# Layer 1's table products in a two-layer cross-attention kernel: two 64-row tiles of the array in place of a block-diagonal operand

## The reference, cut to what matters

```
a = layer_norm(ctx)                      # 64 keys per batch
K = a @ Wk.T ; V = a @ Wv.T              # 16 heads of 64
scores = (x @ Wq.T) K^T / 8              # per head
out = softmax(scores) V @ Wo.T
return x + tanh(gate) * out
```

## Time and profile before

| | us |
|---|---|
| median of 3 runs | 1936.01 (1934.52 to 1938.28) |
| the profiled execution, device time | 1932.28 |
| its span | 1930.5 |
| PE busy in the span | 1826.7 (95%) |
| DVE, ACT, POOL busy | 1082.6, 585.9, 1032.3 |

### The profile page before, as it was taken

How to read it: one execution, slowest core, us unless ns; L and a number is a source line. 1 busy time by engine, 2 the same in 40 slices (tenths; PEclk the granted TensorE clock), 3 DMA queues, 4 the chain that set the end, 5 groups by cost and what they waited for, 6 DMA issues and landing times.

```text
span 1930.5 us, 22356 instructions
## 1 busy us (share of the span) xinstructions
PE 1826.7 (95%) x8640; PEld 1509.4 (78%) x8640; DVE 1082.6 (56%) x1086; ACT 585.9 (30%) x680; POOL 1032.3 (53%) x580
## 2 busy tenths in 40 slices
PE   5999999999988899999999977999999999999998
PEld 5788888888876777888778856887788778877887
DVE  6888888888867444444344456335633563356342
ACT  3444444444434332233332323112211221122111
POOL 2677777777758755465544656225522552255221
PEclk9999999999999999999999989999999999999999
DMA  8423333233163475655756554422342234132110
GB/s 204 108 76 82 83 79 78 74 81 85 45 191 111 131 235 201 198 180 175 242 188 211 189 189 153 152 77 83 136 153 66 100 118 153 66 118 101 66 55 33
DMA packets 249961, 244.43 MB, mean 127 GB/s; under 512 B 61440, under 2 KB 204928, under 8 KB 249856
## 3 DMA queue, kind: packets, MB, share of 16 engines
q1 hardware_dynamic: 248704, 241.97, 39.9%
q10 hardware_dynamic: 1152, 1.05, 0.2%
HBM read 157.99 MB, written 84.93 MB: 126 GB/s over the span
## 4 chain that ended last, share of the span: by engine, by line
PE 56%; DVE 19%; issue 9%; ACT 6%; POOL 4%; DMA 3%; SPq 2%; ACTq 0%; DVEq 0%; POOLq 0%
PE ps L53 18%; PE ps L55 18%; PE ps L54 18%; DVE small L972 4%; DVE pr L995 3%; ACT pr L741 3%; DVE pT1r L1006 2%; DVE pT0r L1006 2%; PE ps L648 2%; ACT ot L735 2%; DVE xT0r L902 1%; DVE xT1r L902 1%; POOL prob L1280 1%; DVE x2r L1075 1%; DMA xb<-in_x_dram 1%
## 5 line engine op out<-in xcount | busy, mean ns | idle before, releaser
L1275 POOL TENSOR_TENSOR prob<-prob,small 128x1024 f32<-128x1024 f32 x32 | 61.0, 1908 | 397.0 <-DVE small L1086 397.0
L1206 POOL TENSOR_TENSOR pr<-pr,small 128x1024 f32<-128x1024 f32 x64 | 122.0, 1906 | 100.0 <-DVE small L1001 100.0
L1082 DVE SCALAR_TENSOR_TENSOR prob<-ps,bias 128x1024 f32<-128x1024 f32 x32 | 39.1, 1222 | 227.6 <-PE ps L55 227.6
L840 ACT CAST x2Th<-x2r 128x1024 fp32r<-128x1024 f32 x32 | 33.6, 1050 | 424.6 <-DVE x2r L1075 424.6
L1227 POOL TENSOR_TENSOR xb<-xb,bo 128x1024 f32<-128x1024 f32 x32 | 79.9, 2497 | 141.0 <-DMA xb<-in_x_dram 141.0
L1201 POOL TENSOR_TENSOR pr<-pr,small 128x1024 f32<-128x1024 f32 x64 | 124.0, 1938 | 34.8 <-DVE small L976 34.6
L1050 DVE TENSOR_TENSOR y<-ps,xb 128x512 f32<-128x512 f32 x64 | 44.0, 687 | 159.3 <-PE ps L55 156.4
L972 DVE TENSOR_REDUCE small<-pr 128x16 f32<-128x1024 f32 x64 | 78.1, 1220 | 91.0 <-ACT pr L741 91.0
L53 PE MATMUL ps<-wo0h,oc0l 128*128 128x512 f32 x256 | 101.6, 397 | 0.0
L53 PE MATMUL ps<-wo0h,oc1l 128*128 128x512 f32 x256 | 101.0, 395 | 0.0
L53 PE MATMUL ps<-xT0h,wq0l 128*128 128x512 f32 x256 | 100.7, 393 | 0.0
(11 more groups left out here) (320 smaller groups left out, 5583.1 us busy)
## 6 DMA issues: line engine op xcount, KB each, us to landing
o_scratch<-ot SPq DMA_DIRECT2D x256, 64.0 KB, 1.8
ocr<-o_scratch SPq DMA_DIRECT2D x16, 1024.0 KB, 6.2
xb<-in_x_dram SPq DMA_DIRECT2D x32, 512.0 KB, 6.0
x_scratch<-y SPq DMA_DIRECT2D x32, 512.0 KB, 3.5
a_scratch<-ost SPq DMA_DIRECT2D x64, 256.0 KB, 3.0
b_scratch<-ost SPq DMA_DIRECT2D x64, 256.0 KB, 2.5
xd<-x_scratch SPq DMA_DIRECT2D x128, 128.0 KB, 2.8
raw<-b_scratch SPq DMA_DIRECT2D x32, 512.0 KB, 8.0
```

The lines of the kernel that those rows point to most:

```text
L1206: nc.gpsimd.tensor_tensor(heads(v), heads(v), mx.unsqueeze(2).to_broadcast([P, TPB * GRP, KEYS]), ALU.subtract)\
L1275: nc.gpsimd.tensor_tensor(prob[:], prob[:], mx1.unsqueeze(2).to_broadcast([P, H1, KEYS]), ALU.subtract)\
```

## The change

The two heads of a pair are no longer put in one product with zeros. `bd` holds only the blocks, [128, BATCH, KEYS]: partitions 0 to 63 are head 0, 64 to 127 head 1. Each product is issued as two matmuls over 64 partitions each, one per head, alternating, into separate banks. The 16 products of a pair f become 8 rounds r: r < 4 makes two column tiles e of table A (per e: 3 terms x 2 heads, 256 columns each), r >= 4 makes two batches and half of Wo's columns of table B (3 terms x 2 heads, 512 columns each). A round has two banks, and the rounds alternate between V and TT, so four banks are used; before writing, a round waits for the evictions of the round before the last. ACT evicts head 0's bank and DVE head 1's, for r < 4 with a strided write that puts the heads side by side. The transposes into TT and the first scores wait for the evictions, and round 1 for Wo's turned rows. `diagonal` is one instruction instead of two; POOL's zeroing and its wait go. The stores keep their number and size.

```diff
-        bd = [[at(f"bd{i}{x}", 180 + 4 * i + 2 * j, [P, BATCH, 2, KEYS], F32R) for j, x in enumerate("hl")]
+        bd = [[at(f"bd{i}{x}", 180 + 4 * i + 2 * j, [P, BATCH, KEYS], F32R) for j, x in enumerate("hl")]
-        ost = [at(f"ost{i}", 188 + 2 * i, [P, HALF]) for i in range(4)]
+        ost = [at(f"ost{i}", 188 + 4 * i, [P, 2, HALF]) for i in range(2)]
-        X = V
+        X = [V, [TT[:, HALF * i:HALF * (i + 1)] for i in range(2)]]
...
@@ store_outer
-                sp.wait_ge(evac_d if o % 2 else evac_a, 8 * f + o // 2 + 1)
+                tile = ost[o // 2 % 2][:, o % 2]
+                if i == 0 or o % 2 == 0:
+                    sp.wait_ge(evac_a, 8 * f + o // 2 + 1)
+                if i == 0 or o % 2 == 1:
+                    sp.wait_ge(evac_d, 8 * f + o // 2 + 1)
...
@@ table_part, s == 0
-                        after(pe, wo1_lo, f)
+                        after(pe, evac_a, 8 * f)
+                        after(pe, evac_d, 8 * f)
@@ table_part, s >= 3
-                    for o in range(4 * (s - 3), 4 * (s - 2)):
...
+                    for r in range(2 * (s - 3), 2 * (s - 2)):
+                        if r == 0:
                             pe.wait_ge(o_ev, UNITS)
                             pe.wait_ge(bd_lo, 2 * f + 1)
                             pe.wait_ge(w1_lo, f + 1)
+                        if r in (1, 4):
                             pe.wait_ge(bd_lo, 2 * f + 2)
                             pe.wait_ge(wo1_lo, f + 1)
-                        after(pe, evac_d if o % 2 else evac_a, 8 * f + o // 2)
-                        if i == 0:
-                            a_ = [wqs[x][:, e] for x in (0, 1)]
-                            b_ = [bd[0][x][:].rearrange("p b h s -> p (b h s)") for x in (0, 1)]
-                        else:
-                            a_ = [bd[1][x][:, e // 2].rearrange("p h s -> p (h s)") for x in (0, 1)]
-                            b_ = [woT[x][:, HALF * (e % 2):HALF * (e % 2 + 1)] for x in (0, 1)]
-                        three(nc, X[o % 2], a_, b_, True, True).then_inc(outer, 1)
+                        after(pe, evac_a, 8 * f + r - 1)
+                        after(pe, evac_d, 8 * f + r - 1)
+                        head = [slice(HD1 * h, HD1 * (h + 1)) for h in range(2)]
+                        terms = ((1, 0), (0, 1), (0, 0))
+                        for e in range(2 * r, 2 * r + 2) if r < 4 else ():
+                            for j, (x, y_) in enumerate(terms):
+                                for h in range(2):
+                                    last = nc.tensor.matmul(X[r % 2][h][:, CTX * (e % 2):][:, :CTX], wqs[x][head[h], e],
+                                                            bd[0][y_][head[h]].rearrange("p b s -> p (b s)"),
+                                                            start=j == 0, stop=j == 2)
+                                    if e % 2 == 1 and j == 2:
+                                        last.then_inc(outer, 1)
+                        for j, (x, y_) in enumerate(terms) if r >= 4 else ():
+                            q, n = divmod(r - 4, 2)
+                            for h in range(2):
+                                last = nc.tensor.matmul(X[r % 2][h], bd[1][x][head[h], 2 * q:2 * q + 2].rearrange("p b s -> p (b s)"),
+                                                        woT[y_][head[h], HALF * n:HALF * (n + 1)], start=j == 0, stop=j == 2)
+                                if j == 2:
+                                    last.then_inc(outer, 1)
...
@@ ACT out_slot
-                    for o in range(4 * (s - 3), 4 * (s - 2), 2):
-                        act.wait_ge(outer, 16 * f + o + 1)
-                        after(act, ost_st[o % 4], 16 * (4 * f + o // 4))
-                        nc.scalar.copy(ost[o % 4][:], X[0]).then_inc(evac_a, 1)
+                    for r in range(2 * (s - 3), 2 * (s - 2)):
+                        act.wait_ge(outer, 16 * f + 2 * r + 1)
+                        for i in range(2 if r < 4 else 1):
+                            after(act, ost_st[2 * (r % 2) + i], 16 * (4 * f + r // 2))
+                        if r < 4:
+                            nc.scalar.copy(ost[r % 2][:].rearrange("p e (b h s) -> p e b h s", b=BATCH, h=2)[:, :, :, 0],
+                                           X[r % 2][0].rearrange("p (e b s) -> p e b s", e=2, b=BATCH)).then_inc(evac_a, 1)
+                        else:
+                            nc.scalar.copy(ost[r % 2][:, 0], X[r % 2][0]).then_inc(evac_a, 1)
...
@@ POOL slot
-                if u == UNITS + 3:
-                    pool.wait_ge(pv, UNITS)
-                    for i in range(2):
-                        for x in range(2):
-                            nc.gpsimd.memset(f32(bd[i][x][:]), 0.0).then_inc(bd_zero, 1)
```

More of the change, by code:

```diff
@@ L182, in program @@
         (wo_hi, wo_lo, c_ld, oc_hi, oc_lo, o_done, xbo, y_done, st_done, aggr, coef, applied, scaled, normed,
-         bd_zero, wt_turned, wT_hi, wT_lo, w1_hi, w1_lo, wo1_turned, wo1_hi, wo1_lo, proj, bd_hi, bd_lo, outer, evac_a,
+         wt_turned, wT_hi, wT_lo, w1_hi, w1_lo, wo1_turned, wo1_hi, wo1_lo, proj, bd_hi, bd_lo, outer, evac_a,
          evac_d) = (sem(n) for n in (
-             "wo_hi wo_lo c_ld oc_hi oc_lo o_done xbo y_done st_done aggr coef applied scaled normed bd_zero "
+             "wo_hi wo_lo c_ld oc_hi oc_lo o_done xbo y_done st_done aggr coef applied scaled normed "
              "wt_turned wT_hi wT_lo w1_hi w1_lo wo1_turned wo1_hi wo1_lo proj bd_hi bd_lo outer evac_a evac_d").split())
@@ L308, in store_outer @@
                 i, e = divmod(o, 8)
-                sp.wait_ge(evac_d if o % 2 else evac_a, 8 * f + o // 2 + 1)
+                tile = ost[o // 2 % 2][:, o % 2]
[3 more added lines that the diff above has]
+                    sp.wait_ge(evac_d, 8 * f + o // 2 + 1)
                 if i == 0:
                     sp.dma_start(d["a"][:, P * e:P * (e + 1), P * f:P * (f + 1)].rearrange("b p c -> p b c"),
-                                 ost[o % 4][:].rearrange("p (b c) -> p b c", b=BATCH)).then_inc(ost_st[o % 4], 16)
+                                 tile.rearrange("p (b c) -> p b c", b=BATCH)).then_inc(ost_st[o % 4], 16)
                 else:
-                    b, n = divmod(e, 2)
-                    sp.dma_start(d["b"][b, P * f:P * (f + 1), HALF * n:HALF * (n + 1)], ost[o % 4][:])\
+                    q, n = divmod(e // 2, 2)
+                    rows = P * f + HD1 * (o % 2)
+                    sp.dma_start(d["b"][2 * q:2 * q + 2, rows:rows + HD1, HALF * n:HALF * (n + 1)], tile)\
                         .then_inc(ost_st[o % 4], 16)
@@ L587, in table_part @@
                 else:
-                    for o in range(4 * (s - 3), 4 * (s - 2)):
-                        i, e = divmod(o, 8)
-                        if o == 0:
+                    for r in range(2 * (s - 3), 2 * (s - 2)):
+                        if r == 0:
                             pe.wait_ge(o_ev, UNITS)
@@ L593, in table_part @@
                             pe.wait_ge(w1_lo, f + 1)
-                        if o == 8:
+                        if r in (1, 4):
                             pe.wait_ge(bd_lo, 2 * f + 2)
                             pe.wait_ge(wo1_lo, f + 1)
-                        after(pe, evac_d if o % 2 else evac_a, 8 * f + o // 2)
-                        if i == 0:
-                            a_ = [wqs[x][:, e] for x in (0, 1)]
-                            b_ = [bd[0][x][:].rearrange("p b h s -> p (b h s)") for x in (0, 1)]
-                        else:
-                            a_ = [bd[1][x][:, e // 2].rearrange("p h s -> p (h s)") for x in (0, 1)]
-                            b_ = [woT[x][:, HALF * (e % 2):HALF * (e % 2 + 1)] for x in (0, 1)]
-                        three(nc, X[o % 2], a_, b_, True, True).then_inc(outer, 1)
+                        after(pe, evac_a, 8 * f + r - 1)
[17 more added lines that the diff above has]
+                                    last.then_inc(outer, 1)
             def logits(u):
@@ L608, in logits @@
                 if u == 0:
-                    pe.wait_ge(wo1_lo, KT)
+                    pe.wait_ge(evac_a, 8 * KT)
+                    pe.wait_ge(evac_d, 8 * KT)
                 if u == 1:
@@ L778, in diagonal @@
                 after(act, outer, 16 * (f - 1) + 8 * (i + 1))
[L779 to L782, removed]
+                nc.scalar.copy(bd[i][0][:].rearrange("p b (r i) -> p b r i", r=2),
+                               PJ[i].rearrange("p (r b i) -> p b r i", r=2, b=BATCH)).then_inc(bd_hi, 1)
             def out_slot(h):
@@ L787, in out_slot @@
                     act.wait_ge(pv, UNITS)
-                    act.wait_ge(bd_zero, 4)
                 f, s = table(h - 1)
@@ L1020, in diagonal @@
                 dve.wait_ge(bd_hi, 2 * f + i + 1)
[L1021 to L1025, removed]
+                nc.vector.tensor_tensor(bd[i][1][:].rearrange("p b (r i) -> p b r i", r=2),
```

(11 more changed lines are left out.)

## The result

The changed kernel takes 2126.44 us (median of 4 runs, 2123.12 to 2128.39), the kernel before 1935.59: a ratio of 1.099, 95% interval 1.0974 to 1.1006. The forecast was 1914.8, in a range of 1888 to 1934.

The account below looks back on a forecast made before the run. PE was taken to bound the table stage, busy 474.8 of 477 us. Outer parts falling from 104.4 to 82.9 us gave 21.5, less 0.3 waited away at the stage's end: 1936.0 - 21.2 = 1914.8 us, range 1888 to 1934.

Parts of the forecast that it names:

- Stores keep their bytes.: Clause on the table stores, listed among the edits that cost nothing: 0 us.
- D: Rival: the tiles' matmuls run one after the other, plus mode changes; 3 us more, 1939; chance 0.12.
- E: Rival: each alternation between tiles empties the array like a mode change; 67 us more, 2003; chance 0.04.
- The stalls: In each outer part, PE's eviction waits of 0.55 us (table A) and 0.38 (table B) go with four banks.
- Columns: Outer-part matmul time: from no overlap, 2.88 (table A) and 2.73 us (B), to full overlap, 1.44 and 1.36.
- Weight loads: In outer parts, the tiles' loads pass one after the other: table A 2.72 us a part, table B 1.36.
- rival B: The tiles also load beside each other, table A parts at 1.44 us; 42 us less, 1894.3; chance 0.26.
- Rival C: A load waits until its own tile's matmul is over, table B parts 2.0 us; 11 less, 1925; chance 0.12.
- The changes of mode: Switching between whole array and tiles, twice a part, 64 times: 0.275 us each, 0.55 a part, 17.6 in all.
- The sum on PE: All 32 outer parts on PE: 82.9 us against 104.4, 21.5 less.
- None is near: In the table stage no other engine is close to having no slack; POOL, the busiest other, has 45% idle.
- A: The forecast itself: tiles multiply side by side, loads pass one after the other; 1914.8 us, chance 0.40.

Follow-up runs that it names:

- f2: Changed kernel with the values' columns in the order key, batch, so a table B store has 64 keys outermost and 2 batches inside: 1909.57 us.
- f3: Kernel before, each table B product stored to 64 rows of two batches instead of 128 rows of one: 2155.57 us.
- f6: Kernel before, each table B product stored to 32 rows of all four batches, outermost dimension 4: 2004.15 us.
- g1: f2 with POOL computing the layer norm's coefficients before the low part of the next chunk instead of after: 1888.72 us.
- f4: Kernel before, still block-diagonal operands and whole-array matmuls, but products go round four banks (V and TT) instead of two: 1918.15 us.
- f5: f2 with the three products of one head issued before the three of the other instead of alternating, both tables: 1910.71 us.
- f7: g1 with the six matmuls of one head of a table A round issued before the six of the other: 1894.42 us.

## Why the prediction was wrong

*The step that failed* is one clause among the edits costed at nothing: "Stores keep their bytes." They do, and their shape changed. From the diff, one line of `store_outer`, it could have been asked what the row of a store's dimensions says: 128 rows, against 2 x 64. The price is shown from three sides: the changed kernel without the slow shape is 217 us faster (f2), the old kernel with it is 221 us slower (f3), and with half as slow a shape 70 us slower (f6). The Trainium skill has the rule (DMA: Bandwidth & Descriptors, Why a DMA increments its semaphore by 16 and not by 1): a DMA is spread over the largest number of engines up to 16 that divides the size of the slowest dimension (of those larger than 1) on both of its sides; the shares of 0.13 and 0.26 of 16 engines agree. The prediction weighed pages on TensorE alone.

*Where the time went.* From 645 us to the first scores, the changed kernel takes 687.8 us (to 1332.75) and g1, which has the same matmuls, 454.6 (to 1099.62). Of these 233 us, 163 are PE's idle time in the stage, 33 the longer wait before the first scores (46.8 against 13.9), and 37 are the same matmuls at a lower clock (478.0 us busy against 440.7).

My slower rivals, D and E, put the loss on PE. Of the sentence on what would prove me wrong, "if PE waited for another engine in the stage", the wait came, but by the transposes more than by round 1: PE waited 15.3 us for `bd1l` before round 1, three times, and 100.1 for `ost`. "The transposes at s = 0 wait for round 7's evictions, which have a half tile too" was the sentence that failed with the stores.

*The stalls*: right. f4 alone gave 16.7 us against 17. But the list of DVE's work beside them (residual, statistics and two copies, under 3 us) leaves out the multiplication by gamma, which waits for ACT.

*Columns*: the halving is shown in both tables. The upper bound, no overlap, is out.

*Weight loads*: wrong by 20.5 us, on the good side. I let the tiles' loads pass one after the other, 2.72 us for a part of A; it took 1.62 with its way out. In the timeline with PE's loads (PEld), the two tiles' loads are one row, and the next pair of loads comes 0.11 later:

```profile
680.69 0.19 PEld L609 LDWEIGHTS ps<-bd0h,wqsl 64*128 64x128 f32 x2 [0.35 <-issue]
680.80 0.19 PEld L609 LDWEIGHTS ps<-bd0l,wqsh 64*128 64x128 f32 x2
```

That is rival B's mechanism, which I gave 0.26. The 0.11 us of the earlier trace rows was the time of a load on one tile, and I read it as the time between any two. The Trainium skill says (TensorEngine Tiling (Array Packing), Key Properties) that different tiles can load weights and multiply in parallel; these rows agree. Rival C, a load that waits for its own tile's matmul, would have shown pairs 0.33 apart in table B; they are 0.23 apart (863.01, 863.24).

*The changes of mode*: there, and cheaper than taken. On the way in, 0.32 passes from the last whole-array matmul to the first tile's (680.37 to 680.69) instead of 0.2275, and 0.11 for its uncovered load (680.69 to 680.91 is 0.22 against 0.12): 0.20 us. On the way out, a part's last pair to the next half tile is 0.33 (863.93 to 864.26) instead of 0.2275, and its load 0.11: 0.21. With 0.41 a part against 0.55, 32 parts cost 13 us and not 17.6. The tile's first load starts (680.69) before the last matmul's modelled end (680.76), which I had waited for in the sum; as that end is a model, the rows give the price of the change and don't say whether the array had emptied.

*The sum on PE*, then: 16 x (12 x 0.12 + 0.41) + 16 x (6 x 0.2275 + 0.41) = 29.6 + 28.4 = 58.0 us, against 104.4: 46.4 less, not 21.5. g1, with stores and coefficients in order, is 45.9 us under the kernel before in its runs (1934.6 to 1888.7). That it is so near is in part luck: the profiled spans differ by 44.1, since g1 stands 2.5 us longer before the first scores.

*"None is near", of the other engines*: wrong by a queue, not by busy time. It cost f2 20.9 us (1909.57 to 1888.72). The sign was in the rows: PE waited three times on a late eviction of DVE, and the same view of the kernel before has

```profile
DVE y L1017 <- ACT y L774: 49.3, 22, 7.6
```

I had counted busy time; but DVE's evictions stand behind a chain over POOL and ACT, and with shorter half tiles and the transposes waiting on evictions, PE pays for it.

*A slip of arithmetic*: A, B, C and two thirds of the others add up to a chance of 0.82 and not 0.80.

*Still open*: how much of PE's idle time each late issue behind the slow stores causes was not taken apart; 64 stores of 5.1 us are 328 us of two engines' time, part of it hidden. And g1 ends its stage where it should, but waits a little longer before the first scores, 13.9 us against 11.39, which was not tried.

## What to carry to other kernels

When an edit changes what a tile holds, write down the dimensions of every DMA that reads or writes it, before and after, and not its bytes alone: the outermost one decided here how many engines carried it, and the issues behind it in the same queue came late. A wait of the bounding engine can cost more than its length, where the clock has fallen after it (37 us here). Before calling an engine idle, follow what its next buffer-freeing instruction stands behind in its own queue; a gain on the bounding engine turns slack in that order into the next bound. Zeros in a block-diagonal operand are worth removing with row tiles: two heads run for the price of one, plus 0.4 us for each visit to the tiled mode.

## What the runs showed of the hardware

- A DMA store of 256 KB in packets of 2 KB kept as many engines busy as its outermost dimension had entries: 2 entries 0.13 of 16 and 51 GB/s, 4 entries 0.26 and 95 GB/s. With 64 entries, 390 GB/s were moved in all, other transfers included.
- Behind such stores with 2 entries, single issues of SP took 2.6 to 5.6 us; the store's own issue took 3.48 us at the median, 0.32 in the kernel before.
- While PE stood still from 790 to 800 us of the changed kernel, the granted clock was 0.50, and after another such wait the matmuls of 512 columns came 0.43 us apart instead of 0.23 (882 to 886 us, granted clock 0.50), the lower of the two levels, 1.2 GHz for 2.4.
- Two 64-row tiles load weights and multiply side by side in fp32r: one pair of 256 columns in 0.12 us, one of 512 in 0.23.
- Entering and leaving the tiled mode cost 0.20 and 0.21 us.
- PE runs matmuls of the two tiles in pairs even when three of one tile are issued before three of the other (1.62 us a part), and with six apart leaves three without a partner (1.96): in both, a matmul started ahead of two of the other tile that were issued before it. The Trainium skill (TensorE: Matmul & The Clock Gate, Part 3) has matmuls start strictly in the order of issue; f5 and f7 disagree for matmuls on different tiles.
